# Rotation of queries and keys in the first attention: one stacked product, one multiply, one add across partition halves, and the low half made by VectorE

## The reference

```python
def _apply_rope_subspace(x, d_rope):
    e, o = (xr[..., 0::2], xr[..., 1::2])
    rot = jnp.stack([e * cos - o * sin, e * sin + o * cos], axis=-1).reshape(xr.shape)
...
    h = (x - mu) * jax.lax.rsqrt(var + LN_EPS) * ln_scale + ln_bias
    c_q = h @ w_down_q.T
    c_kv = h @ w_down_kv.T
    q = (c_q @ w_up_q.T).reshape(b, s, H, DH).transpose(0, 2, 1, 3)
    k = (c_kv @ w_up_k.T).reshape(b, s, H, DH).transpose(0, 2, 1, 3)
    v = (c_kv @ w_up_v.T).reshape(b, s, H, DH).transpose(0, 2, 1, 3)
    q = _apply_rope_subspace(q, DR)
    k = _apply_rope_subspace(k, DR)
    scores = jnp.einsum('bhqd,bhkd->bhqk', q, k) * scale
    attn = jax.nn.softmax(scores, axis=-1)
    out = jnp.einsum('bhqk,bhkd->bhqd', attn, v)
    out = out.transpose(0, 2, 1, 3).reshape(b, s, H * DH)
    out = out @ w_out.T + residual
```

## Time and profile before

| | before |
|---|---|
| median of 3 runs | 2263.4 us (2263.2 to 2265.54) |
| span of the profiled execution | 2263.8 us |
| PE busy | 2100.6 us (93%) |
| POOL busy | 1828.5 us (81%) |
| DVE busy | 1789.1 us (79%) |
| ACT busy | 1732.0 us (77%) |

### The profile page before, as it was taken

The page is one execution under the profiler, slowest core; times in us unless marked ns, Lnnn a source line. Parts: engine busy times, 40 slices in busy tenths (PEclk is TensorE's granted clock), DMA queues, the critical chain, the costliest instruction groups (busy, mean ns, idle before and its releaser), DMA issues. The chain is left out here.

```text
span 2263.8 us, 56900 instructions
## 1 busy us (share of the span) xinstructions
PE 2100.6 (93%) x22674; PEld 1263.2 (56%) x22674; DVE 1789.1 (79%) x3457; ACT 1732.0 (77%) x3507; POOL 1828.5 (81%) x1239
## 2 busy tenths in 40 slices
PE   5899999999999999999999989986999899988878
PEld 1466666666666666666666646652454444444444
DVE  7788888888888888888888658978868986887214
ACT  5798898998989988988989945657566775775543
POOL 4899999999999999999999945627777777777720
PEclk9999999999999999999999989978579996999878
DMA  4000000000000000000000000111211111111101
GB/s 153 1 2 2 2 2 2 2 2 2 2 2 2 2 2 2 2 2 2 2 2 2 2 15 23 39 39 27 52 38 32 38 33 38 31 38 36 39 10 37
DMA packets 44688, 43.19 MB, mean 19 GB/s; under 512 B 21312, under 2 KB 33424, under 8 KB 44176
## 3 DMA queue, kind: packets, MB, share of 16 engines
q1 hardware_dynamic: 28560, 23.35, 3.6%
q0 software_dynamic: 15872, 16.28, 3.1%
HBM read 33.83 MB, written 1.57 MB: 16 GB/s over the span
## 5 line engine op out<-in xcount | busy, mean ns | idle before, releaser
L380 POOL TENSOR_TENSOR probs_lo<-probs,probs_hi 128x1024 f16<-128x1024 f32 x512 | 1076.7, 2129 | 43.0 <-ACT probs L430 42.6
L494 DVE TENSOR_REDUCE part_max<-aux 128x1 f32<-128x512 f32 x1024 | 677.9, 687 | 91.0 <-PE aux L568 86.7
L429 ACT ACTIVATE probs_hi<-scores 128x512 f16<-128x512 f32 x1024 | 630.2, 615 | 134.6 <-PE scores L601 117.3
L430 ACT ACTIVATE probs<-scores 128x512 f32<-128x512 f32 x1024 | 636.6, 622 | 0.0
L1622 POOL DMA_INDIRECT far<-key_table,placeT x456 | 451.9, 991 | 142.9 <-issue 138.7
L617 PE MATMUL acc<-v,probs_hi 128*128 128x65 f16 x4096 | 451.1, 193 | 2.3 <-POOL probs_lo L380 2.3
L619 PE MATMUL acc<-v,probs_hi 128*128 128x64 f16 x4096 | 452.3, 195 | 0.0
L621 PE MATMUL acc<-v,probs_lo 128*128 128x65 f16 x4096 | 450.6, 192 | 0.0
L617 PEld LDWEIGHTS acc<-v,probs_hi 128*128 128x128 f16 x4096 | 382.5, 96 | 82.6 <-POOL probs_lo L380 2.5
L619 PEld LDWEIGHTS acc<-v,probs_hi 128*128 128x128 f16 x4096 | 380.0, 97 | 75.5
L568 PE MATMUL aux<-k_a,q_a 128*128 128x512 f16 x1024 | 392.1, 383 | 5.2 <-DVE roped L480 2.1
(11 more groups left out here) (329 smaller groups left out, 3935.5 us busy)
## 6 DMA issues: line engine op xcount, KB each, us to landing
far<-key_table,placeT POOLq DMA_INDIRECT x496, 2.4
qT<-qT SPq DMA_DIRECT2D x16, 256.0 KB, 2.9
e_w<-in_e_w SPq DMA_DIRECT2D x48, 64.0 KB, 1.9
x<-in_x SPq DMA_DIRECT2D x4, 256.0 KB, 3.9
cos<-in_cos SPq DMA_DIRECT2D x1, 1024.0 KB, 6.8
sin<-in_sin SPq DMA_DIRECT2D x1, 1024.0 KB, 8.9
e_w<-in_e_w SPq DMA_DIRECT2D x2, 512.0 KB, 3.9
out<-x SPq DMA_DIRECT2D x4, 256.0 KB, 2.7
```

The source lines that it names most:

```text
L380: pool.tensor_tensor(probs_lo[:, slot], probs[:, wide], probs_hi[:, slot], ALU.subtract).then_inc(low_ready, 1)
L429: act.activation(probs_hi[:, slot, i], bank, ACT.Exp, scale=float(DH0) ** -0.5)
L430: act.activation(probs[:, wide, i], bank, ACT.Exp, scale=float(DH0) ** -0.5).then_inc(probs_ready, 1)
L494: dve.tensor_reduce(part_max[g % 2][:, n % QT, n // QT:n // QT + 1], bank, AX.X, ALU.max).then_inc(aux_free, 1)
```

## The change

A rotation takes one aux unit. The weights are stacked: columns 0 to 63 of a head are in even-odd order, 64 to 127 in swapped order, so one product gives both parts, one above the other in the partitions. The table `turns` has the cosines in partitions 0 to 63 and the signed sines in 64 to 127; DVE multiplies once into `rope_term` and adds partitions 0 to 63 and 64 to 127 of it into `roped`, now 64 partitions. `wq_sw`, `wk_sw` and their loads and halves go, and one table is loaded instead of two. ACT copies `roped` in two instructions of 64 partitions for queries and keys alike. The subtraction for the low half leaves POOL's queue and goes into DVE's, at the same due time of 3.5 steps behind the rotation.

```diff
@@ -305,8 +304,7 @@
     for h in range(H0):
         for c in range(NCH):
             g, end = NCH * h + c, KPAIR * (NCH * h + c + 1) + LAG
-            for kind in "kq":
-                plan += [(rope_at(kind, h, c), "rope", (kind, h, c, part)) for part in range(2)]
+            plan += [(rope_at(kind, h, c), "rope", (kind, h, c)) for kind in "kq"]
             plan += [(KPAIR * g - 12.5 + n / 2, "max", (g, n)) for n in range(NCH * QT)]
             plan += [(KPAIR * g - 3.5, "shift", g), (end, "norm", g)]
             plan += [(end + 1.5, "turn", g), (end + 3, "out", g)] if h % 2 else []
...
@@ -366,14 +364,6 @@
         with nc.Block() as block:
             @block.gpsimd
             def _(pool):
-                def rope_low(r):
-                    kind, h, c = ropes[r]
-                    a, b, cols = chunk(kind, h, c)
-                    dst = a if kind == "k" else b
-                    pool.wait_ge(hi_ready, r + 1)
-                    pool.tensor_tensor(dst[0:LAT0, cols], roped[r % ROPED][0:LAT0, :], a[0:LAT0, cols], ALU.subtract
-                                       ).then_inc(lo_ready, 1)
-
                 def low_half(n):
                     slot, wide = n % SLOTS, n % WIDE
                     pool.wait_ge(probs_ready, 2 * n + 2)
...
@@ -392,14 +382,11 @@
                     pool.wait_ge(xa_full, 1)
                     pool.tensor_tensor(x[:], x[:], keep["xa"][:], ALU.add).then_inc(x_ready, 1)
 
-                work = [(math.floor(rope_at(*rope)) + 3.5, "rope", r) for r, rope in enumerate(ropes)]
-                work += [(n + 1, "low", n) for n in range(ALL)]
+                work = [(n + 1, "low", n) for n in range(ALL)]
                 work += [(WEIGHTS_AT + 1.25 + i, "weight", i) for i in range(len(WEIGHTS))]
                 work += [(RESIDUAL_AT + 1.25, "residual", 0)]
                 for _, kind, n in sorted(work):
-                    if kind == "rope":
-                        rope_low(n)
-                    elif kind == "weight":
+                    if kind == "weight":
                         weight_low(n)
                     elif kind == "residual":
                         residual()
...
@@ -411,10 +398,9 @@
                 def high_halves(r):
                     kind, h, c = ropes[r]
                     a, b, cols = chunk(kind, h, c)
-                    act.wait_ge(aux_free, unit_no["rope", (kind, h, c, 1)] + 1)
-                    if kind == "k":
-                        act.activation(b[0:LAT0, cols], roped[r % ROPED][0:LAT0, :], ACT.Copy)
-                    act.activation(a[:, cols], roped[r % ROPED][:], ACT.Copy).then_inc(hi_ready, 1)
+                    act.wait_ge(roped_ready, r + 1)
+                    act.activation((b if kind == "k" else a)[0:DH0, cols], roped[r % ROPED][:], ACT.Copy)
+                    act.activation(a[DH0:, cols], roped[r % ROPED][:], ACT.Copy).then_inc(hi_ready, 1)
 
                 def exponentials(n):
                     slot, wide = n % SLOTS, n % WIDE
...
@@ -465,20 +451,15 @@
                     bank = aux[u % AUX][:]
                     dve.wait_ge(aux_full, u + 1)
                     if kind == "rope":
-                        of, h, c, part = arg
-                        r = rope_no[of, h, c]
-                        cols = slice(c * CH, (c + 1) * CH)
-                        if part == 0:
-                            dve.tensor_tensor(term[r % 2][:], bank, keep["cos"][:, cols], ALU.mult
-                                              ).then_inc(aux_free, 1)
-                        else:
-                            dve.tensor_tensor(bank, bank, keep["sin"][:, cols], ALU.mult).then_inc(rope_turned, 1)
-                            if r >= ROPED:
-                                dve.wait_ge(lo_ready, r - ROPED + 1)
-                            dve.wait_ge(aux_free, unit_no["rope", (of, h, c, 0)] + 1)
-                            dve.wait_ge(rope_turned, r + 1)
-                            dve.tensor_tensor(roped[r % ROPED][:], bank, term[r % 2][:], ALU.add
-                                              ).then_inc(aux_free, 1)
+                        c, r = arg[2], rope_no[arg]
+                        dve.tensor_tensor(term[r % 2][:], bank, keep["turns"][:, c * CH:(c + 1) * CH], ALU.mult
+                                          ).then_inc(aux_free, 1)
+                        if r >= ROPED:
+                            dve.wait_ge(lo_ready, r - ROPED + 1)
+                        dve.wait_ge(aux_free, u + 1)
+                        dve.tensor_tensor(roped[r % ROPED][:], term[r % 2][0:DH0, :], term[r % 2][DH0:, :], ALU.add
+                                          ).then_inc(roped_ready, 1)
+                        dve.wait_ge(roped_ready, r + 1)
                     elif kind == "v":
                         h, half = arg
                         if h >= 2:
...
@@ -504,6 +485,14 @@
                         rows = x[:, QT * c:QT * c + QT, :].rearrange("p t d -> p (t d)")
                         dve.tensor_tensor(rows, rows, bank, ALU.add).then_inc(aux_free, 1)
 
+                def rope_low(r):
+                    kind, h, c = ropes[r]
+                    a, b, cols = chunk(kind, h, c)
+                    low, high = (a, b) if kind == "k" else (b, a)
+                    dve.wait_ge(hi_ready, r + 1)
+                    dve.tensor_tensor(low[0:DH0, cols], roped[r % ROPED][:], high[0:DH0, cols], ALU.subtract
+                                      ).then_inc(lo_ready, 1)
+
                 def negated_maxima(g):
 
                     dve.wait_ge(aux_free, unit_no["max", (g, NCH * QT - 1)] + 1)
...
@@ -521,12 +510,15 @@
                                       inv[g % 2][:].unsqueeze(2).broadcast_to([P, QT, DH0]), ALU.mult
                                       ).then_inc(norm_ready, 1)
 
-                dve.wait_ge(keep["rope_in"], 2 * 16)
+                dve.wait_ge(keep["rope_in"], 16)
                 work = [(at, 0, kind, arg) for at, kind, arg in units]
                 work += [(KPAIR * g - 4.9, 1, "reduce", g) for g in range(H0 * NCH)]
+                work += [(math.floor(rope_at(*rope)) + 3.5, 1, "low", r) for r, rope in enumerate(ropes)]
                 for _, _, kind, arg in sorted(work, key=lambda w: w[:2]):
                     if kind == "reduce":
                         negated_maxima(arg)
+                    elif kind == "low":
+                        rope_low(arg)
                     elif kind == "norm":
                         normalise(arg)
                     else:
...
@@ -541,8 +533,8 @@
                     if u >= AUX:
                         pe.wait_ge(aux_free, u - AUX + 1)
                     if kind == "rope":
-                        of, h, c, part = arg
-                        w = keep[("wq", "wq_sw", "wk", "wk_sw")[2 * (of == "k") + part]][:, h * P:(h + 1) * P]
+                        of, h, c = arg
+                        w = keep["w" + of][:, h * P:(h + 1) * P]
                         hi, lo = (keep["cq1"], keep["cq2"]) if of == "q" else (keep["ck1"], keep["ck2"])
                         cols = slice(c * CH, (c + 1) * CH)
                         if h == 2 and c == 0:
...
@@ -2180,8 +2171,7 @@
     angle = np.outer(np.arange(T, dtype=f32), inv)
     cos = np.concatenate([np.cos(angle), np.cos(angle)], -1)[:, ::2].T.astype(f32)
     sin = np.concatenate([np.sin(angle), np.sin(angle)], -1)[:, ::2].T.astype(f32)
-    t["cos0"] = np.ascontiguousarray(np.tile(cos, (4, 1)))
-    t["sin0"] = np.ascontiguousarray(np.tile(np.concatenate([-sin, sin], 0), (2, 1)))
+    t["turns0"] = np.concatenate([cos, cos, -sin, sin], 0)
 
     theta = (1.0 / 10000.0 ** (2.0 * np.arange(HALF1, dtype=f32) / f32(ROPE1))).astype(np.float64)
     place = np.arange(T)
...
@@ -2222,9 +2212,9 @@
     odd_even = np.concatenate([np.arange(1, DH0, 2), np.arange(0, DH0, 2)])
     twice = lambda w, axis: np.concatenate([w, w], axis)
 
-    def up(w, order):
-        w = w.reshape(H0, DH0, LAT0)[:, order, :].transpose(2, 0, 1)
-        return twice(twice(w, 2).reshape(LAT0, H0 * P), 0)
+    def up(w):
+        w = w.reshape(H0, DH0, LAT0).transpose(2, 0, 1)
+        return twice(np.concatenate([w[:, :, even_odd], w[:, :, odd_even]], 2).reshape(LAT0, H0 * P), 0)
 
     m = {
         "x": a["L0_attn_x"].reshape(T, D),
```

More of the change, by code:

```diff
@@ L115, in allocators @@
             lambda n: ctx.enter_context(nc.semaphore(n)))
-WEIGHTS = ("wq", "wq_sw", "wk", "wk_sw", "wv")
+WEIGHTS = ("wq", "wk", "wv")
 def first_heads(w):
@@ L337, in heads @@
         term = [sb(f"rope_term{i}", [P, CH], F32) for i in range(2)]
-        roped = [sb(f"roped{i}", [P, CH], F32) for i in range(ROPED)]
+        roped = [sb(f"roped{i}", [DH0, CH], F32) for i in range(ROPED)]
         part_max = [sb(f"part_max{i}", [P, QT, NCH], F32) for i in range(2)]
@@ L357, in heads @@
         unit_no = {w: n for n, w in enumerate(banked)}
-        ropes = [arg[:3] for kind, arg in banked if kind == "rope" and arg[3] == 0]
```

(1 more changed line is left out.)

18 lines of the change are left out of this document (7 added, 11 removed).

## The result

The changed kernel takes 2320.1 us (median of 4 runs, 2318.2 to 2321.2), the kernel before 2264.5 us beside it (4 runs, 2263.2 to 2269.0): a ratio of 1.0244, 95% interval 1.023 to 1.0259. It is slower by 56 us, where the forecast was 51 us.

What follows compares the result with a forecast made beforehand. PE was taken as the bound now, DVE after the change: 17.0 work + 3.0 waits + 0.3 bunching = 20.3 us a block, 0.8 more, x 64 = +51 on 2263.8: 2315 us. Range for 8 in 10: 2235 to 2410 us.

Steps and rivals of the forecast that it cites:

- PE's gain: Rotations lose two matmuls each, 0.86 us a block: PE's bound falls from 19.5 to 18.65, worth 55 us if alone.
- DVE's own work: DVE's work a block without waits for POOL stays nearly the same, 16.9 + 0.04, say 17.0 us.
- Four waits of 0.76: DVE's two adds and two low halves a block, both inputs in SBUF, each wait 0.76 us for POOL: 3.0 us.
- If DVE comes at any moment: Assumption pricing DVE's wait for POOL at random phase: 0.79 us on average, 0.76 once the block is longer.
- The rival on the other side: Faster: fixed phase puts DVE's four waits late in POOL's instruction or its pause, below 0.5 us each; chance 0.22.
- The bunching: DVE's work and waits fall together in about one step, PE runs dry of banks: 0.3 us a block added.
- ACT, +0.5 us a block, hidden: One more 64-partition query copy brings ACT to 18.0 us a block, below 18.65, hidden by its waiting for scores.
- partitions don't count: ACT's 64-partition and 128-partition copies both take 0.52 us, so the added copy was priced at +0.5 us a block.
- POOL's loss: POOL loses 0.5 to 2.8 us a block beside DVE, reaching 17.2 to 19.5 us, not binding beside DVE's 20.3.
- The start: Ahead of the first scores, head 0's low halves share DVE with rotations: nothing, give or take 5 us.
- The forecast's own range: DVE bound by waits for POOL of 0.6 to 1.1 us each: 2270 to 2385 us, chance 0.54.
- What the profile after would show: PE about 91% busy, add and low half 1.2 to 1.5 us, singles up to 2.7, POOL's count about 118.

Runs made afterwards that it cites:

- e12: The change with POOL subtracting only 64 of 1024 columns a step and the high half's second copy by DMA instead of ACT: -50 us to before, ratio 0.9793.
- e8: The kernel before with ACT's two 64-partition copies as in the change: +24 us to before, ratio 1.0113.
- e11: The change with the high half's second copy by DMA instead of on ACT: +34 us to before, ratio 1.0101.
- e7: The change with the first weights' subtractions on POOL five steps later: +49 us to before, ratio 1.0224.
- e5: The change with POOL's 128x1024 subtraction split into two instructions of 128x512: +61 us to before, ratio 1.027.
- e1: The kernel before with the sine product written to SBUF, so the add has both inputs in SBUF: +385 us to before, ratio 1.1418.
- e4: The change with the rotation's low half back on POOL: +202 us to before, ratio 1.0761.
- e2: The change with an add that reads one half from PSUM, one more DVE instruction per rotation: +44 us to before, ratio 1.0183.
- e9: e2 with e7's edit and the high half's second copy by DMA instead of on ACT: -4 us to before, ratio 0.9988.

## Why the prediction was right

The result, the bound of the gain and the main cause were right. That the forecast came within 5 us is luck in part, since two errors cancelled.

- **PE's gain, 0.86 us a block, bound 18.65.** Right: 18.71 in e12, with all else out of the way. The 2209 us that it would give are 2263.8 - 55, and e12 gained 50.
- **DVE's own work, 17.0 us.** Right: busy 278.5 / 300 x 20.41 = 18.9 us a block, less 2.2 of waits is 16.7.
- **Four waits of 0.76, 3.0 us.** Right in kind, too large: the adds wait 1526 - 690 = 0.84 us each, the queries' low half 1207 - 674 = 0.53, the keys' nothing, 2.2 us in all. "If DVE comes at any moment" was the step that failed: each of the four comes at a phase of its own in every block. The rival on the other side had named this, and one of four places did land in the pause.
- **The bunching, 0.3 us.** Too small: DVE is idle 1.5 us a block (20.41 - 18.9). PE waits for DVE after a long add, 25.6 us before the fills of maxima and 36.3 before "shift" in the stretch, and then DVE for PE (47.0 us), and ACT's copies come on top. So DVE binds by when it is late and not by being full, and "shift", which the prediction didn't name, is the place where PE feels it most. With 17.0 + 2.2 + 0.3 = 19.5 the forecast would have been no change; that the sum came out right, 20.3 against 20.4, is luck in its parts.
- **ACT, +0.5 us a block, hidden.** Wrong twice: 1.02 us (e8), and 0.36 to 0.68 us of the block (e11, e12). The failed step read "partitions don't count" from copies that stayed in their partitions, and took room in ACT's mean as cover; PE waits for ACT for 19.5 us in the stretch where it had waited for 0.2, although ACT is idle for 9% of it.
- **POOL's loss, 0.5 to 2.8 us.** Inside: 8 x (2228 - 2128) ns = 0.8 us. Where an add got in between two instructions of POOL the next took 2.58 us and not 2.13 (median; 79 adds of 114 over 0.9 us). POOL lost 0.45 us to an operation that ran on for 0.55, more than the half that the row of the first experts had shown. The Trainium skill (SBUF — State Buffer, Who interferes with whom) has the later one fully blocked; these runs are near it on both sides. It did not make POOL the bound: PE and ACT waited for none of its results.
- **The start, 0 give or take 5.** Just outside: 6.3 us (e7).
- **The forecast's own range, 2270 to 2385 us for waits of 0.6 to 1.1 us.** The ends aren't summed alike: with the 0.3 us of bunching they would be 19.7 and 21.7 us a block, about 2277 and 2405 us. It decides nothing here.
- **What the profile after would show.** PE 91% was 93%, DVE's waiting groups at 1.2 to 1.5 us were 1.53, 1.21 and 0.69, single ones "up to 2.7" were 2.5, POOL's count "about 118" 119.

Open: when DVE gets in between two queued instructions of POOL. In the change 79 of 114 long adds did, in e5 all 106, in e1 3 of 112, in e4 43 of 100, while in e1 61 and in e4 29 let one to three whole ones by. The runs differ in the add's partitions, in POOL's instructions and in when the next becomes ready; none of them changes one of these alone.

## What to carry to other kernels

Before an operation of VectorE gets both inputs in SBUF beside long GpSimd instructions of the same kind, price each place by its phase in GpSimd's queue, not by an average: here the same kind of read cost nothing, 0.5 or 0.8 us in the change and 2.7 us in e1. Keep one input in PSUM where it is there anyway, even at the price of one more instruction (e2 by 12 us, e9 against e11 by 38, some 5 of them from e7's edit), and look at what stands right behind that instruction in the queue: here a short one that TensorE was waiting for. And when a change frees the bound, add what it puts on every other link of the chain, measured on an instruction of exactly that form: here PE gave 50 us (e12), and the waits for GpSimd and ScalarE's copies took 106. A wait list of the bound engine names the links; shares of busy time don't.

## What the runs showed of the hardware

- A VectorE operation of 512 columns with both inputs in SBUF that waits for GpSimd is done 0.55 us behind the end of a GpSimd instruction, where it takes 0.69 us alone, and can let up to three whole queued ones by; the longest add of e4 took 7.84 us in place of 0.69.
- A ScalarE copy of 64x512 from partitions 0 to 63 into 64 to 127 began 0.63 us behind its predecessor and kept its successor off for 0.66, in place of 0.52 (e8).
- Where GpSimd waited its turn behind VectorE, its instruction took 2.58 us in place of 2.13 (the change).
- A DMA of 64 KB from SBUF to SBUF landed 1.9 us from its issue (e9), beside four engines at 88 to 97%.
